# Spreading the last row chunk's layer-1 tiles among the remaining layer-2 tiles of a two-layer graph kernel

## The reference

```python
h = maximum(layernorm(x), 0)
mask = (adj < 0.5) & ~eye;  r = where(mask, adj, 1)
S = where(mask, exp(-(1/r - 1/mu)**2 / (2*sigma**2)), 0)
x = x + S @ (h @ W0 + B0)              # layer 1
h = maximum(layernorm(x), 0)
x = x + (adj*adj + eye) @ (h @ W1.T)   # layer 2
```

## Time and profile before

| | us |
|---|---|
| median of 3 runs | 1984.09 |
| the 3 runs | 1981.47, 1984.09, 1987.01 |
| the profiled execution: its own time | 1984.96 |
| the profiled execution: span | 1983.0 |
| TensorE busy | 1890.0 (95%) |
| ScalarE busy | 1676.4 (85%) |
| VectorE busy | 1666.8 (84%) |
| share of the chain that ended last: ScalarE, TensorE, VectorE | 64%, 18%, 8% |
| tile loads: number, size, median to landing | 418, 1024 KB, 6.6 |

### The profile page before, as it was taken

How to read it: one execution, slowest core, us unless ns; L and a number is a source line. 1 busy time by engine, 2 the same in 40 slices (tenths; PEclk the granted TensorE clock), 3 DMA queues, 4 the chain that set the end, 5 groups by cost and what they waited for, 6 DMA issues and landing times.

```text
span 1983.0 us, 12915 instructions
## 1 busy us (share of the span) xinstructions
PE 1890.0 (95%) x4576; PEld 844.2 (43%) x4576; DVE 1666.8 (84%) x937; ACT 1676.4 (85%) x963; POOL 0.5 (0%) x5
## 2 busy tenths in 40 slices
PE   7988989999999999999999999999999999999997
PEld 4543333344444444444444444444444444443333
DVE  7999999999999999999999999999999963333343
ACT  7999999999999999999999999999999972222210
POOL 0000000000000000000000000000000000000000
PEclk9999999999999999999999999999999999999999
DMA  6565666768787867676655564656464646677865
GB/s 263 186 229 198 230 259 260 270 258 303 276 307 289 332 233 305 266 286 248 250 207 212 204 235 172 233 190 244 170 233 154 239 177 259 277 297 290 329 256 212
DMA packets 87471, 487.59 MB, mean 246 GB/s; under 512 B 9968, under 2 KB 10352, under 8 KB 33904
## 3 DMA queue, kind: packets, MB, share of 16 engines
q1 hardware_dynamic: 87408, 486.78, 64.9%
HBM read 464.72 MB, written 22.02 MB: 245 GB/s over the span
## 4 chain that ended last, share of the span: by engine, by line
ACT 64%; PE 18%; DVE 8%; issue 5%; DMA 4%; SPq 0%; DVEq 0%
ACT rings L666 20%; ACT rings L676 19%; ACT rings L671 19%; PE p_x L418 12%; ACT rings L683 4%; DMA rings<-adjT 4%; PE p_l1b L404 3%; DVE rings L562 2%; DVE rings L544 2%; DVE rings L551 2%; PE p_own L418 2%; DVE xa_buf L630 1%; DMA x_buf<-xT 1%; ACT rstd_buf L712 0%; ACT rstd_buf L710 0%
## 5 line engine op out<-in xcount | busy, mean ns | idle before, releaser
L551 DVE SCALAR_TENSOR_TENSOR rings<-rings,small 128x2048 f32<-128x2048 f32 x256 | 601.3, 2349 | 59.8 <-ACT rings L671 59.1
L418 PE MATMUL p_x<-rings,h 128*128 128x512 f32 x1296 | 580.3, 600 | 28.6 <-ACT rings L683 12.6
L544 DVE SCALAR_TENSOR_TENSOR rings<-rings 128x2048 f32<-128x2048 f32 x256 | 585.8, 2288 | 0.6
L562 DVE TENSOR_TENSOR rings<-rings 128x2048 f32<-128x2048 f32 x174 | 398.3, 2289 | 198.0 <-DMA rings<-adjT 140.2
L676 ACT ACTIVATE rings<-rings,small 128x2048 f32<-128x2048 f32 x256 | 533.5, 2084 | 4.0 <-DVE rings L551 4.0
L666 ACT ACTIVATE rings<-rings,small 128x2048 f32<-128x2048 f32 x256 | 509.8, 1991 | 7.5 <-DVE rings L544 6.8
L404 PE MATMUL p_l1b<-rings,h 128*128 128x512 f32 x1024 | 465.7, 599 | 28.7 <-ACT rings L676 28.6
L671 ACT ACTIVATE rings<-rings 128x2048 f32<-128x2048 f32 x256 | 488.1, 1907 | 5.0
L404 PE MATMUL p_l1a<-rings,h 128*128 128x512 f32 x1024 | 463.2, 597 | 13.5 <-ACT rings L676 12.7
L418 PEld LDWEIGHTS p_x<-rings,h 128*128 128x128 f32 x1296 | 247.8, 192 | 348.5 <-issue 348.0
L683 ACT ACTIVATE rings<-rings 128x2048 f32<-128x2048 f32 x82 | 156.1, 1904 | 246.3 <-DMA rings<-adjT 190.9
(11 more groups left out here) (63 smaller groups left out, 244.5 us busy)
## 6 DMA issues: line engine op xcount, KB each, us to landing
rings<-adjT SPq DMA_DIRECT2D x418, 1024.0 KB, 6.6
xa_buf<-acc_dram SPq DMA_DIRECT2D x57, 256.0 KB, 7.0
acc_dram<-xa_buf SPq DMA_DIRECT2D x52, 256.0 KB, 2.2
x_buf<-xT SPq DMA_DIRECT2D x32, 256.0 KB, 4.6
outT<-xa_buf SPq DMA_DIRECT2D x16, 256.0 KB, 2.3
acc_dram<-y_buf SPq DMA_DIRECT2D x15, 256.0 KB, 2.8
y_buf<-acc_dram SPq DMA_DIRECT2D x11, 256.0 KB, 7.8
acc_dram<-x_buf SPq DMA_DIRECT2D x1, 256.0 KB, 2.2
```

Source lines behind the costliest of these rows:

```text
L418: last = pe.matmul(out[:, :], h2[:, it.source * G + g, :], block_of(q_ring, it.m % Q_RING, g), start=(it.first and g == 0), stop=(it.last ...
L544: dve.scalar_tensor_tensor(out=tile(s_ring, t % S_RING), in0=tile(a_ring, slot), scalar=CUTOFF, in1=tile(a_ring, slot), op0=ALU.is_lt, op1 ...
L551: dve.scalar_tensor_tensor(out=v, in0=v, scalar=neg_2c, in1=v, op0=ALU.add, op1=ALU.mult).then_inc(squared, 1)
L562: squares = dve.tensor_tensor(tile(q_ring, it.m % Q_RING), a, a, ALU.mult)
```

## The change

- `QUOTA` becomes 0, 5, 9, 11, then 12 for chunks 4 to 14 (before 0, 4, 7, 9, 12...). The early chunks take 5 items more in all.
- Chunk 15 has no quota: all items left but `TAIL` = 7 plus one per row are spread over its 16 steps. It holds 76 items (12 own, 64 in chains) among its 16 layer-1 tiles; 23 items follow it, one per step: 7 with source 14, then the 16 with source 15, each a final chain of one item.
- Non-final chains: 65 instead of 52, chains in all 81 instead of 68, tile loads 422 instead of 418, state loads 70 instead of 57. Between chunks 4 and 8 chains of two and more replace most chains of one: 17 chains end there instead of 30; in chunks 9 to 14 it is 11 instead of 9. The chain with index 56 is the first of an unbroken run of chains of one item, 56 to 80 (items 231 to 255).
- Chain work is placed by item number m, not by step. VectorE adds a chain after item `last_m + 3` (final: `last_m + 1`), never before the chain ahead of it; SP stores it after the load of item `evac + 5` and loads a state after the load of the item given below.
- From step 240 on items are squared by ScalarE if m is odd, else by VectorE (before: from step 256 on); row work comes ahead of the items of a step in chunks 15 and 16.
- `load_prior` moves from place 10 to place 13 of a chunk.

```diff
-QUOTA = [0, 4, 7, 9] + [12] * 12
+QUOTA = [0, 5, 9, 11] + [12] * 11
+TAIL = 7
+EVAC = 3
+STEAL = 0.5
...
+def slots_of(c):
+    if c == 1:
+        n = QUOTA[1]
+        return [H2_STEP + k * (NC - H2_STEP) // n for k in range(n)]
+    if c < NC - 1:
+        n = QUOTA[c]
+        return [(2 * k + 1) * NC // (2 * n) for k in range(n)]
+    n = NC * NC - NC - sum(QUOTA) - TAIL
+    return [(2 * k + 1) * NC // (2 * n) for k in range(n)] + [NC + k for k in range(TAIL)]
...
+    ends = [Chain(row, [J for J in range(NC) if (row, J) not in done], True) for row in range(NC)]
+    ends.sort(key=lambda ch: -len(ch.sources))
...
-    if it.step >= S_STEPS:
+    if it.step >= S_STEPS - NC:
         it.by = "act" if it.m % 2 else "dve"
...
+for ch in CHAINS:
+    ch.evac = max(ch.last_m + (1 if ch.final else EVAC), CHAINS[ch.index - 1].evac if ch.index else 0)
+    ch.store = ch.evac + A_RING
+    EVAC_AFTER.setdefault(min(ch.evac, len(ITEMS) - 1), []).append(ch)
+    STORE_AFTER.setdefault(ch.store, []).append(ch)
+    if state_before(ch) is not None:
+        free = CHAINS[ch.index - XA_RING].store if ch.index >= XA_RING else 0
+        free = max([free, ch.first_m] + [o.store for o in ch.before])
+        own = [it.m for it in ITEMS if it.step >= (ch.row + 1) * NC + 9]
+        if ch.begin >= (ch.row + 1) * NC:
+            free = max(free, own[0])
+        LOAD_AFTER.setdefault(free, []).append(ch)
...
+            def chains_after(m):
+                for ch in STORE_AFTER.get(m, []):
+                    store_chain(ch)
+                for ch in LOAD_AFTER.get(m, []):
+                    load_state(ch)
...
+                for it in AT_STEP[s]:
+                    if it.load >= n:
+                        load_tile(it.load)
+                        n = it.load + 1
+                    chains_after(it.m)
...
                 for it in AT_STEP[s]:
                     if it.by == "dve":
                         square_adj(it)
+                    for ch in EVAC_AFTER.get(it.m, []):
+                        add_chain(ch)
```

More of the change, by code:

```diff
@@ L23, with __init__ @@
 TINY = 2.0 ** -60
-QUOTA = [0, 4, 7, 9] + [12] * 12
+QUOTA = [0, 5, 9, 11] + [12] * 11
 S_STEPS = NC * NC
 H2_STEP = 9
+TAIL = 7
+EVAC = 3
+STEAL = 0.5
 class Chain:
-    def __init__(self, index, row, sources, final):
-        self.index, self.row, self.sources, self.final = index, row, sources, final
+    def __init__(self, row, sources, final):
+        self.row, self.sources, self.final = row, sources, final
 class Item:
@@ L42, in __init__, with next_chain @@
         self.own = chain is None
-def best_row(c, limit, done):
+def slots_of(c):
[7 more added lines that the diff above has]
+    return [(2 * k + 1) * NC // (2 * n) for k in range(n)] + [NC + k for k in range(TAIL)]
+def next_chain(c, places, done):
     found = None
+    late = places[0] >= H2_STEP
+    limit = c if late else c - 1
     for row in range(NC):
+        if row == c or row == c - 1 and not late:
+            continue
         left = [J for J in range(limit) if (row, J) not in done]
-        if row in (c - 1, c) or not left:
+        if not left:
             continue
-        key = (row < c, len(left), -row if row < c else row)
+        key = -(STEAL * (row > c) + 1 / len(left)), -row if row < c else row
         if found is None or key > found[0]:
@@ L54, in best_row @@
     return found
[L57 to L66, removed]
-def make_plan():
[L70 to L80, removed]
-            chains.append(chain)
[L82 to L94, removed]
-        rest = iter(J for J in range(NC) if J not in own)
[L96 to L106, removed]
@@ new lines, in make_plan @@
+def make_plan():
+    done, chains, items, order = set(), [], [], [list(range(NC))]
+    for c in range(1, NC):
+        places = slots_of(c)
+        own = [J for J in range(c) if (c, J) not in done][-len(places):]
+        steps = sorted({i for i in places if i < NC})
+        own_at = {steps[(2 * k + 1) * len(steps) // (2 * len(own))]: J for k, J in enumerate(own)}
+        own_at.pop(max(own_at))
+        own_at[NC - 1 if NC - 1 in steps else steps[-1]] = own[-1]
+        done.update((c, J) for J in own)
+        free, picked, taken = [], [], set()
+        for i in places:
+            if i in own_at and i not in taken:
+                taken.add(i)
+                picked.append((i, c, own_at[i], None))
+            else:
+                free.append(i)
+        while free:
+            _, row, left = next_chain(c, free, done)
+            left = left[:len(free)]
+            chain = Chain(row, left, False)
+            chains.append(chain)
+            done.update((row, J) for J in left)
+            picked += [(i, row, J, chain) for i, J in zip(free, left)]
+            free = free[len(left):]
+        rest = iter(J for J in range(NC) if J not in own)
+        order.append([own_at[i] if i in own_at else next(rest) for i in range(NC)])
+        picked.sort(key=lambda p: p[0])
+        items += [Item(row, J, chain, c * NC + i) for i, row, J, chain in picked]
+    ends = [Chain(row, [J for J in range(NC) if (row, J) not in done], True) for row in range(NC)]
+    ends.sort(key=lambda ch: -len(ch.sources))
+    chains += ends
+    tail = [(ch, J) for ch in ends for J in ch.sources]
+    items += [Item(ch.row, J, ch, S_STEPS + TAIL + k) for k, (ch, J) in enumerate(tail)]
+    for k, ch in enumerate(chains):
+        ch.index = k
@@ L107, in make_plan @@
     return chains, items, order
 CHAINS, ITEMS, ORDER = make_plan()
-STEPS = S_STEPS + len([it for it in ITEMS if it.step >= S_STEPS])
+STEPS = ITEMS[-1].step + 1
 AT_STEP = [[] for _ in range(STEPS + 8)]
@@ L149 @@
     mine = [it for it in ITEMS if it.chain is ch]
-    ch.begin, ch.end, ch.last_m = mine[0].step, mine[-1].step, mine[-1].m
+    ch.begin, ch.end, ch.first_m, ch.last_m = mine[0].step, mine[-1].step, mine[0].m, mine[-1].m
     ch.before = [x for x in CHAINS[:ch.index] if x.row == ch.row]
@@ L179 @@
 PRIORS = [c for c in range(NC) if prior_of(c) is not None]
+EVAC_AFTER, STORE_AFTER, LOAD_AFTER = {}, {}, {}
+for ch in CHAINS:
[9 more added lines that the diff above has]
+            free = max(free, own[0])
+        assert free <= ch.evac + A_RING - 1, (ch.row, ch.sources, free, ch.evac)
+        LOAD_AFTER.setdefault(free, []).append(ch)
 def gnn_program(nc, xT, adjT, W0, B0, mu, sigma, W1T, outT):
@@ L366, in _ @@
             n = 2
-            for s in range(STEPS + 8):
+            for s in range(STEPS):
                 c, i = divmod(s, NC)
-                for ch in CHAINS:
-                    if s == ch.end + (3 if ch.final else 5):
-                        store_chain(ch)
                 if c >= 1 and i == 8 and c <= NC:
@@ L377, in _ @@
                     load_residual(c)
-                if i == 10 and c in PRIORS:
+                if i == 13 and c in PRIORS:
                     load_prior(c)
[L380 to L389, removed]
+                if s < S_STEPS and S_LOAD[s] >= n:
+                    load_tile(S_LOAD[s])
+                    n = S_LOAD[s] + 1
+                for it in AT_STEP[s]:
[3 more added lines that the diff above has]
+                    chains_after(it.m)
                 if 2 <= s < NC:
                     load_nodes(s)
+            for m in range(len(ITEMS), CHAINS[-1].store + 1):
+                chains_after(m)
         @block.tensor
@@ L630, in add_chain, with row_steps @@
                     dve.tensor_tensor(buf[:, :], p_x[k % 2][:, :], buf[:, :], ALU.add).then_inc(xa_added, 1)
+            def row_steps(c, i):
+                if c > NC:
+                    return
+                if i == 3:
+                    add_x1(c - 1)
+                if i == 4 and c >= 2:
+                    add_y(c - 1)
+                if i == 7:
+                    norm_row(c - 1)
             for s in range(STEPS + 8):
@@ L637, in _ @@
                     premask(s)
+                if c >= NC - 1:
+                    row_steps(c, i)
                 for it in AT_STEP[s]:
@@ L646, in _ @@
                         constants()
[L647 to L656, removed]
+                if 1 <= c < NC - 1:
+                    row_steps(c, i)
         @block.scalar
@@ L717, in keep_h2, with row_steps @@
                                ACT.Copy).then_inc(h2_ready, 1)
+            def row_steps(s):
+                c, i = divmod(s, NC)
+                if i == 5 and c <= NC:
+                    square_row(c - 1)
+                if i == 6 and c <= NC:
+                    rstd_row(c - 1)
+                if i == 8 and c < NC or s == S_STEPS + 7:
+                    keep_h2(c - 1)
             for s in range(STEPS + 8):
@@ L728, in _ @@
                     log(s)
+                if c >= NC - 1:
+                    row_steps(s)
                 for it in AT_STEP[s]:
```

## The result

The changed kernel takes 1972.03 us in the median (1971.25 to 1973.96), the kernel before 1984.09; the ratio is 0.9941, interval 0.9927 to 0.9956. The forecast was 1967: faster, by 17 us where 12 were measured. The profiled execution took 1971.93 us, with a span of 1970.2, 12.8 less than before.

A forecast was written before the change was run, and what follows sets the result against it. TensorE was taken to bound the tail. TensorE's end with parts 1 to 3 at 1925.0, plus 36.5 (loop), 1.5 (clock) and 3.2 (end), gave span 1966.2; +1.96 outside, -0.87 for the median: 1967, range 1928 to 1983.

The forecast's parts named there:

- What bounds the kernel: TensorE and ScalarE full from chunk 4 on, VectorE too in chunk 4; after 1624 us only TensorE has work.
- part 3: Chunk 15 with 76 items: TensorE stays full, needing 316 us, with 2.9 us to spare per step.
- The starting point: Chunk 14's last product, put at 1530.6, with 119 tiles of 3.435 us remaining; old tail loses 34.9 us.
- Part 1: Five more items in chunks 1 to 3: 17.2 us leave the later part, 1.8 us early cost, net -15.4.
- Part 2: Fewer chains in chunks 4 to 8 relieve VectorE: -4.5 us (ends 0 and -5.5); chunks 9 to 14 cost 0.
- the 1928 of the prediction: Span with parts 1 to 3 alone: TensorE's end at 1925.0 plus 3.2 us behind the last product.
- Part 4: Last 25 items: SP's state load waits for a store behind a tile load; loop of 16 turns, 6.45 us each, +36.5.
- the clock's 1.5: Tail, once TensorE pauses: its clock grant falls as in the old tail, +1.5 us.
- A: End of item 232 at TensorE's own pace; last product at A + 88.6 without the wait, A + 125.1 with it.
- B: Rival: in the tail, SP's store lands regardless of the tile ahead, so the turn is hidden: about 1931; chance 0.18.
- C: Rival: the middle gives nothing, Part 2 is 0 and early items cost VectorE's 9 us: 1981; chance 0.10.
- D: Rival: slower, same state-load wait, store landing in 8.5 us, turn 9.4: 2014, deciding from turn 7.9; chance 0.09.

The follow-up runs named there:

- e7: Changed kernel with the old quota 4, 7, 9 for chunks 1 to 3, so five more items fall into chunk 15: 1987.0 us.
- f1: The changed kernel itself, run again on one chip beside three variants of it: 1972.99 us, ratio 0.9936.
- f4: Changed kernel with store ahead of the tile load, eight state buffers (layer-1 ring of 6), state load two items after its awaited store: 1928.00 us, ratio 0.9710.
- e1: Changed kernel with each item's store ahead of the tile load on SP's queue instead of behind it: 1939.28 us, ratio 0.9762.
- e2: Changed kernel with store, wait and state load all ahead of the item's tile load: 1970.86 us.
- e5: Changed kernel with each state load one item later than the store it waits for: 1943.55 us, ratio 0.9834.
- e3: Changed kernel with eight state buffers instead of four, layer-1 ring 6 instead of 7: 1946.6 us, ratio 0.9798.

## Why the prediction was right, and where its size was off

*What bounds the kernel, and part 3 (chunk 15):* right. TensorE was busy 320.00 of 320 us.

*The starting point:* misread. The sum counts 119 tiles from chunk 14's last product and puts it at 1530.6, which is VectorE's addition; the product itself ended at 1524.4. So the whole sum starts 6.2 us too late, and the old tail lost 1979.8 - (1524.4 + 408.8 + 5.5) = 41.1 us, not 34.9. TensorE's waits name 29.3 of them (28.5, and 0.8 at 1524 us). The rest, 11.8, is more than matmuls at the lower clock explain by an estimate from its mean grant of 0.97 to 0.98 (7 to 10 us); I have no row for what is left.

*Part 1 (five early items, -15.4):* right in its kind, the early cost too small. 1.8 us were assumed. The changed kernel's own rows have chunk 3's last product 2.8 us later than before, and e7 against it gives 3.5: net -13.7.

*Part 2 (chunks 4 to 8, -4.5):* about half of it came. VectorE's additions give -4.6, but TensorE's own rows -2.6, and chunks 9 to 14 (less 13.7 for the four more items of step 240) cost 0.6 where 0 was set. That fewer chain additions and one VectorE squaring less are the cause was argued from VectorE's fill, which moved by only 1% (98 to 97), and not tried by itself: it stays open. Parts 1 and 2 together bring chunk 14's end, but for the five tiles moved, 0.8 us later (in f1's trace 0.2 earlier), where the sum had 2.7 earlier.

With the sum started at 1524.4 and these 3.5 us put in, the end without a loop is 1922.3, and 1925.5 with the 3.2 behind it; f4's span is 1926.1. That the 1928 of the prediction came within 2 us of f4 is in part luck: 6.2 us too late at the start, 3.5 too much gain in parts 1 and 2.

*Part 4 (the loop):* the mechanism was right, in its place, its members and its range of items; e1, e2 and e5 leave no other reading that I can find. Its size was the mis-sized step: 36.5 us (38 with the clock's 1.5) where the trace shows 45.2. The end of item 232 came at 1833.2, 3.2 earlier than my A of 1836.4 (the two errors above account for 2.7 of that); the last product ended at 1967.0, A + 133.8 with this earlier A, instead of A + 125.1. The 8.7 us fall so:
- Twelve of the sixteen turns took 6.43 on average, against 6.45 assumed: 0.3 less.
- The other four took 35.0 against 28.2 (with the extras that I had given them, +1 for `store_y` and +1.4 for item 247): 6.8 us more. They are the turn with `store_y` in it (6.9) and the one after it (9.4), the turn with the three stores and three state loads of item 247 (9.0) and the one after it (9.7). The extras were taken as work beside an unchanged landing; in truth the megabyte behind such a group landed late, and the store behind it took 8.5 and 8.9 us.
- 1.7 more at the start and 0.5 more at the end.

The sum then closes: +8.7, -3.2 at A, and -1.5 for the clock, which I had booked on top and which lies inside the loop, gives +4.0; the span was forecast at 1966.2 and is 1970.2. The 1967 too is closer than its parts deserve: the late start of the sum hid most of what the loop was too short by. TensorE's waits are only 29.4 of the 45.2; for the other 15.8 its matmuls ran longer, at a mean grant of 0.89 over the last 130 us (14 us by that estimate). In the chain that ended last TensorE is not part of the loop, so this adds nothing of its own.

*The rivals:* B (the turn hidden) did not happen, but f1 and f4 show the price of the wait, 45 us between them, and that DMA allows a tail without it. The Trainium skill (DMA: Bandwidth & Descriptors, Anatomy of one DMA) fits one DMA as 2.0 us plus bytes by 436 GB/s, in a section on transfers that GpSimd issues. That makes 2.6 us for a 256 KB store, where SP's stores took 2.2 in the median. It is no guide to a store behind a megabyte, which the trace decides: 5.4 to 5.8 us in the twelve plain turns. C did not happen as a whole, though half of part 2 failed to come and the early items cost 3.5 us. D did not happen; the turn stayed under 7.9 but for three (9.4, 9.0 and 9.7).

Why a large change moved the time by only 12 us: it removed the 41 us of the old tail, won 16 in the early and middle chunks, and gave 45 back to a wait of SP for a store that it had issued half a microsecond before.

## What to carry to other kernels

When a planner spaces transfers by count, look at every pair in which one waits for the other, and ask what the in-order queue issued between them: nothing between the two means that the whole queue stands still for a full landing, and a large load ahead of the first makes that landing long. A queue's loop is a cycle, so moving a whole group within it changes nothing; moving one member across another does. Check distances for each kind of chain, since one buffer count can be enough for one kind and fall exactly on the wait for another. And count the work of the engine that bounds the kernel from rows of that engine: another engine's row for the same event stood 6 us behind it before the change and 31 us after.

## What the runs showed of the hardware that was not expected

A 1 MB load with two or three 256 KB transfers just ahead of it landed in 8.3 and 8.6 us (issued at 1851.07 and 1901.53 in the changed kernel), not in the 5.3 to 5.6 that it mostly takes there behind one. In the first of the two, the last microseconds are carried by few of the DMA engines, as the tenths of their busy share show in slices of 0.275 us from 1850 on:

```profile
DMA  0000483789998867797967976322212111100000
```

Why engines finish so unevenly stays open, and so does whether the number of transfers ahead is the cause: no run changed it alone. In f4 the DMA engines moved 390 GB/s with a busy share of 0.99, from 1878.85 to 1902.88:

```profile
1878.85:1902.88 24.03, 24.03 (x58) 10.62 (x57) 13.22 (x11) 6.59 (x4) 0.00 (x0) 1.00 0.99 390
```

That is over the 358 GB/s at which the Trainium skill's page (DMA: Bandwidth & Descriptors, Specifications) puts a core's HBM limit, a figure that it derives by dividing a stack's 716 GB/s between two cores; here one core ran. So the case where an item needs 4.4 us did not arise. But it was not far off: at 390 GB/s the 1.57 MB of an item (tile, state, store) take 4.0 us, and in e3 the tile loads came 3.77 us apart with DMA always busy, at 416 GB/s. Both are more than TensorE's 3.435. In those 24 us f4 issued 11.5 MB and moved 9.4, and its tile loads took 10.7 us to land: five tile slots carried the tail over a DMA that was falling behind. A longer run of chains of one would by this estimate be bound by DMA; no run has one.
